# The low parts of eight heads' probabilities are transposed in two transfers of two blocks each instead of one of four

## The reference, cut to what matters

```python
q = split_heads(h @ Wq.T + bq)
k = split_heads(h @ Wk.T + bk)
v = split_heads(h @ Wv.T + bv)
scores = jnp.einsum('bhqd,bhkd->bhqk', q, k) * scale
scores = jnp.where(mask, -jnp.inf, scores)
attn = jax.nn.softmax(scores, axis=-1)
out = jnp.einsum('bhqk,bhkd->bhqd', attn, v)
out = out.transpose(0, 2, 1, 3).reshape(b, n, D_MODEL)
return out @ Wo.T + bo
```

## Time and profile before

| | us |
|---|---|
| median of 3 runs | 1293.63 |
| lowest, highest run | 1293.18, 1296.23 |
| the profiled execution | 1303.47 |
| its span in the trace | 1301.7 |

### The profile page before, as it was taken

The page is one execution under the profiler, slowest core; times in us unless marked ns, Lnnn a source line. Parts: engine busy times, 40 slices in busy tenths (PEclk is TensorE's granted clock), DMA queues, the critical chain, the costliest instruction groups (busy, mean ns, idle before and its releaser), DMA issues.

```text
span 1301.7 us, 39386 instructions
## 1 busy us (share of the span) xinstructions
PE 1163.3 (89%) x15385; PEld 966.6 (74%) x15385; DVE 1046.3 (80%) x2913; ACT 996.1 (77%) x2824; POOL 944.5 (73%) x1606
## 2 busy tenths in 40 slices
PE   3589999989999999999999999999999999999855
PEld 3367877777778777878777887778787788787743
DVE  3478888878888888888888888888888888888752
ACT  2367888788878878878887788778887888788652
POOL 1357777877877787778778777877787778777540
PEclk8689999999999999999999999999999999999996
DMA  5026656676766677766667666676566667665661
GB/s 179 9 50 107 118 114 119 138 123 120 128 131 131 119 135 131 127 120 137 130 110 131 134 129 131 122 132 130 120 134 131 131 120 134 131 130 111 119 115 48
DMA packets 508346, 156.52 MB, mean 120 GB/s; under 512 B 472064, under 2 KB 508160, under 8 KB 508160
## 3 DMA queue, kind: packets, MB, share of 16 engines
q1 hardware_dynamic: 508160, 154.00, 62.4%
HBM read 19.73 MB, written 16.78 MB: 28 GB/s over the span
## 4 chain that ended last, share of the span: by engine, by line
POOL 37%; DVE 24%; ACT 17%; PE 10%; DMA 8%; issue 4%; SPq 1%; POOLq 0%; DVEq 0%
DMA h_t<-h_rows 6%; ACT head_hi L1062 6%; POOL xn L1196 5%; POOL head_lo L1200 4%; POOL head_lo L1206 4%; POOL head_lo L1209 4%; POOL head_lo L1203 4%; DVE h_rows L889 3%; POOL rstd L1189 3%; ACT h_rows L1018 3%; DVE head_nmax L842 3%; DVE head_nmax L838 3%; DVE head_nmax L835 3%; POOL rstd L1220 3%; POOL xn L1193 3%
## 5 line engine op out<-in xcount | busy, mean ns | idle before, releaser
L385 PE MATMUL ps<-w_hi,h_t 128*128 128x256 f16 (+1 forms) x512 | 141.1, 276 | 7.8 <-DMA h_t<-h_rows 7.6
L386 PE MATMUL ps<-h_t,w_hi 128*128 128x256 f16 x512 | 140.9, 275 | 0.0
L387 PE MATMUL ps<-h_t,w_lo 128*128 128x256 f16 x512 | 140.8, 275 | 0.0
L385 PE MATMUL ps<-h_t,w_hi 128*128 128x256 f16 x512 | 140.8, 275 | 0.0
L386 PE MATMUL ps<-w_lo,h_t 128*128 128x256 f16 (+1 forms) x512 | 140.5, 274 | 0.0
L387 PE MATMUL ps<-w_hi,h_t 128*128 128x256 f16 (+1 forms) x512 | 140.2, 274 | 0.0
L385 PE MATMUL ps<-w_hi,agg_hi 128*128 128x256 f16 x512 | 140.1, 274 | 0.0
L386 PE MATMUL ps<-w_lo,agg_hi 128*128 128x256 f16 x512 | 139.7, 273 | 0.0
L387 PE MATMUL ps<-w_hi,agg_lo 128*128 128x256 f16 x512 | 139.4, 272 | 0.0
L1200 POOL TENSOR_TENSOR head_lo<-head_prob,head_hi 128x512 f16<-128x512 f32 x64 | 74.2, 1159 | 84.4 <-ACT head_hi L1062 84.4
L1062 ACT ACTIVATE head_hi<-head_prob 128x2048 f16<-128x2048 f32 x64 | 122.8, 1920 | 0.0
(11 more groups left out here) (192 smaller groups left out, 4956.2 us busy)
## 6 DMA issues: line engine op xcount, KB each, us to landing
x<-in_x SPq DMA_DIRECT2D x64, 256.0 KB, 3.1
out<-x SPq DMA_DIRECT2D x64, 256.0 KB, 2.7
h_t<-h_rows SPq DMA_TRANSPOSE x128, 3.1
head_t_hi<-head_hi SPq DMA_TRANSPOSE x64, 4.6
head_t_lo<-head_lo SPq DMA_TRANSPOSE x64, 4.3
mix_t<-mix_rows SPq DMA_TRANSPOSE x64, 3.0
w_f<-in_w SPq DMA_DIRECT2D x1, 256.0 KB, 2.8
w3t_f<-in_w_t SPq DMA_DIRECT2D x1, 256.0 KB, 3.1
```

Of the source, the lines that this page charges most:

```text
L385: pe.matmul(o, lh, rh, start=start, stop=False)
L386: pe.matmul(o, lh, rl, start=False, stop=False)
L387: return pe.matmul(o, ll, rh, start=False, stop=stop)
```

## The change

The one transfer of `head_lo` becomes two, each with a semaphore of its own. The first moves blocks 0 and 1 into the first eight tiles of `head_t_lo`, the second moves blocks 2 and 3 into the last eight. The first waits for `split_head_1_done`, as the one transfer did; the second has no wait and stands right behind it. PE's `head_sum_1` waits for three semaphores instead of two. POOL's list is the same, line by line.

```diff
-        move_heads_lo_done = [sem(f"move_heads_lo_done_{k}") for k in range(2)]
+        move_heads_lo_a_done = [sem(f"move_heads_lo_a_done_{k}") for k in range(2)]
+        move_heads_lo_b_done = [sem(f"move_heads_lo_b_done_{k}") for k in range(2)]
...
-            def move_heads_lo(g):
+            def move_heads_lo_a(g):
                 sp.wait_ge(split_head_1_done, g + 1)
-                sp.dma_start(head_t_lo[g % 2][:, :, :], head_lo[:, :, :].rearrange("p a n -> p (a n)"), transpose=True).then_inc(move_heads_lo_done[g % 2], 16)
+                sp.dma_start(head_t_lo[g % 2][:, 0:8, :], head_lo[:, 0:2, :].rearrange("p a n -> p (a n)"), transpose=True).then_inc(move_heads_lo_a_done[g % 2], 16)
+
+            def move_heads_lo_b(g):
+                sp.dma_start(head_t_lo[g % 2][:, 8:16, :], head_lo[:, 2:4, :].rearrange("p a n -> p (a n)"), transpose=True).then_inc(move_heads_lo_b_done[g % 2], 16)
...
                 at(4, move_heads_hi)
-                at(4, move_heads_lo)
+                at(4, move_heads_lo_a)
+                at(4, move_heads_lo_b)
...
                 pe.wait_ge(move_heads_hi_done[g % 2], 16 * (g // 2) + 16)
-                pe.wait_ge(move_heads_lo_done[g % 2], 16 * (g // 2) + 16)
+                pe.wait_ge(move_heads_lo_a_done[g % 2], 16 * (g // 2) + 16)
+                pe.wait_ge(move_heads_lo_b_done[g % 2], 16 * (g // 2) + 16)
```

## The result

| | us |
|---|---|
| before, median of 4 runs on the same chip | 1293.41 |
| after, median of 4 runs | 1314.15 (1313.36 to 1315.23) |
| ratio | 1.0156, 95% interval 1.0139 to 1.0174 |
| profiled execution of after, its span | 1315.23, 1313.4 |

The forecast was 1293.7 with a range up to 1299.0. The change costs 20.7 us, and it was put at 0.1. The two profiled executions are only 11.8 apart, since that of before was 9.8 above its median. So the traces are used for where the time goes, and the medians for how much.

A forecast was written before the change was run, and what follows sets the result against it. The prediction saw a ring of waits with POOL most often late. Cost 0 in 62 body groups, 2 x 0.05 = 0.1 in the last two, SP and PE 0, took 1293.63 to 1293.7, range 1290.5 to 1299.

The forecast's parts named there:

- What bounds the kernel: Whole kernel: a ring of waits, POOL most often late with 37% of the chain, all DMA landings 8%.
- The cover of 1.2 on PE: Head sums: low parts ready 1.2 to 1.4 before PE needs them; DVE adds 0.55 before POOL's wait is reached.
- No earlier start: First half's issue: still waits for POOL's fourth subtraction, so gain from overlap with the subtractions is 0.
- Issue on SP: SP's queue: two issues take 2.52, occupying SP 0.62 to 0.84 longer; move3's slack covers it, cost 0.
- The usual landing of the second half: Transfer of head_lo: second half lands 4.3 to 4.4 after the first half's issue, against 4.3 for the one transfer.
- Serial: Rival: second transpose moves nothing until the first lands, 6.1 after issue; +17, 1310.6 us; chance 0.05.
- +0.05: Second half's landing: the delay taken against the one transfer, with bounds from 0 or slightly less to +0.9.
- The third wait: PE's first head sum: a third semaphore wait costs 0, at most some hundredths of a us.
- 8 of the 62 landings come more than 0.6 late: Body groups in before: count used for the held-back rival, whose 0.9 delay passes 6.0 by about 0.1 each, 0.8 together.
- the permitted 6.0: Body groups: a landing costs time only when later than about 5.5 + 0.55, some 6.0, after the issue.
- a shift of the late landings: Rival: changed traffic moves coincidences of late move2 and move3 landings, 4 to 6 us either way, 1288 to 1299; chance 0.11.
- Held back like the high parts: Rival: second half lands at 5.2, +0.9, like the high parts behind other transfers; +2.6, 1296.2 us; chance 0.10.

The follow-up runs named there:

- the first experiment: The changed kernel with both halves counted on one semaphore, so PE has two waits before the head sums: 1312.33, ratio 1.0126 to before.
- whole with PE's packet outside: Kernel before plus 13 matmul pairs per slot and 64 at the start, holding PE's program packets away from the low parts' landing: 1284.08, ratio 0.9919.
- with whole: Kernel before plus 13 matmul pairs per slot and 26 at the start, holding PE's program packets inside the landing's stretch: 1283.11, ratio 0.9909.
- with split: Changed kernel plus 13 matmul pairs per slot and 26 at the start, holding PE's program packets inside the landing's stretch: 1334.66, ratio 1.0305.
- the extra half: Kernel before plus a 128x1024 transfer of constants behind the whole one, nobody waiting for it: 1313.93; with PE's packets held inside, 1327.40.

## Why the prediction was wrong

**What bounds the kernel.** Right. The cover of 1.2 on PE, that of 0.55 on DVE and POOL's wait behind them are the way that the late slots take.

**No earlier start.** Right: the first half is issued at 617.45, when the last subtraction ends.

**Issue on SP.** Right: 1.23 and 1.34 against 2 x 1.24. `move3` stands 4.17 behind the first issue and is not pushed.

**The usual landing of the second half.** Right in size: forecast 4.3 to 4.4 after the first half's issue, measured 4.4 to 4.5 where nothing disturbs. The "Serial" rival (6.1 in every group) is refuted by that: in 40 of 64 groups the two overlap. The Trainium skill's fixed cost per transfer (DMA: Bandwidth & Descriptors, section on the anatomy of one DMA), weighed in the prediction, is not paid twice in a row here: 4.5 for both against 2 x 3.1. One reading behind the +0.05 was loose. `move2` was said to land in 3.1 close behind `move_out`; that is the median of all slots, and in the slot of the earlier trace rows it took 3.5.

**The third wait.** Right, 0 (the first experiment).

**The late landings: the step that failed.** The forecast took "8 of the 62 landings come more than 0.6 late" from the trace of before (it is 7 of the 62, and the eighth is group 62) and carried it over, with at most 0.9 added to each. The sum then had a cost of 0 for 62 groups. In after, 24 of 64 second halves are 0.6 or more late, and they are at 5.8 to 6.7 instead of the permitted 6.0. In before, PE's packet starts in the same stretch in 25 groups, but a whole transfer lands 0.3 later for it, at 4.6, far inside its cover. So the count of late landings in before said nothing of how the new form would meet that packet. I had the late landings under my eyes, and didn't ask what they came from.

The trace shows something there that I overlooked. A second queue called "instruction", q14, has 65 packets of 8 KB in before and in after alike. In all eight late groups of before (4, 9, 17, 25, 38, 43, 56, 62) one of them starts 3.1 to 3.8 behind the last subtraction; in whole with PE's packet outside, all ten landings that are 0.6 or more late (none is over 5.3) have one at 3.7 to 3.9. Group 43 of before has no packet of q8 near; the landing, and window 892.1 to 898.6:

```profile
DMA to landing us min/median/max: 5.1/5.1/5.1
```
```profile
q14 instruction: 1, 0.01, 0.3%
```

In after, where such a packet comes without PE's (groups 4 and 43, at 2.8), the second half is in time, at 5.0 behind the last subtraction. So the eight landings that the forecast counted are marked by another packet than the 24 of after. That the packets of q14 are the cause is not shown: no run moves them, and in before three more groups (30, 35, 51) have one at 3.8 to 3.9 and land at 4.6 to 4.7. Shown is only that one is there at each late landing.

**The rival that came nearest** is "a shift of the late landings": right family, priced at 4 to 6 us from the spread of runs where 20.7 was true, and given 0.11. "Held back like the high parts" had the right sort of size for a delay (+0.9 where +1.2 to 2.1 was measured) but put it on the 8 groups only. The row for it was at hand: the high parts, which do follow close behind others, land as late as 6.3.

**A second term mis-sized.** Beyond 6.0 I counted only the excess, 0.1 per group. In after, the slot of a late group takes 19.21 by the median and that of a punctual one 18.47, so 0.7 is lost, and 1.3 at most. Of this, 0.44 is POOL's `norm2_1`, which goes from 1.06 to 1.50: in 21 of 23 late slots between groups 4 and 59, and in none of the 33 punctual ones. The same instruction has its median at 1.06 with whole and 1.50 with split, both with the packet inside; tile xn of each:

```profile
L1200 POOL TENSOR_SCALAR xn<-x,nmean,rstd x64: 554/1059/1499, 57.4 to 1219.4; 128x256 f32<-128x256 f32 x64
```
```profile
L1206 POOL TENSOR_SCALAR xn<-x,nmean,rstd x64: 554/1498/1506, 57.2 to 1273.0; 128x256 f32<-128x256 f32 x64
```

That the slot jumps by this is shown; why is open. The DVE instructions beside it are the same two in both slots above (lines 872 and 789 of after are lines 866 and 783 of before), only shifted against it, and in before it takes over 1.4 in 14 of 56 slots, without a late landing.

**What stays open.** Why seven groups of after have a packet in the stretch and land punctually. Why a packet of 0.95 us on one DMA engine costs a lone transfer 0.3 and one of a close pair 1.5 to 1.9. In the single groups read packet by packet, the last completion write of a whole transfer stood just ahead of the packet (3.94 and 3.95). In a late group of after the packet was at 4.2 and the last engine's completion write at 5.24, with the landing at 6.29, so there part of the loss is on the way to that write and part behind it. But in a late group with the extra half, the write was at 4.20, just ahead of the packet at 4.21, and the landing at 6.08. The Trainium skill (DMA: Bandwidth & Descriptors, section on queues, rings and completion order) says that the semaphore's write lands only after every earlier write of that engine, across its queues. This would let another queue's packet hold up a landing, but it explains neither sizes above the packet's own 0.95 nor why a lone transfer escapes; no run here tests it. Also open: single whole transfers that land at 6.0 and more (group 25 with the packets inside, and group 62 of before; both have a packet of q14 at 3.8 beside PE's, but so have groups 9, 17 and 56 of before, which land at 5.2), and why the profiled execution of before was 10 us above its median.

## What to carry to other kernels

Slack is not the deadline minus the median landing: count how many landings come late, ask what makes them late, and ask whether the new form of the transfer will meet the same thing worse. In these runs a transposing transfer with another one issued directly at it, waited for or not, was delayed much more by a packet of PE's program than one that stood alone (1.5 to 1.9 against 0.3). A split can win only where the first half can start earlier and somebody waits for the data; here neither was so. In a long unrolled loop like this one the fetch of PE's program is periodic DMA traffic that drifts against the loop: a change of some instructions can move it, so compare two variants at a held position (the loop's PE list padded to whole packets, 512 instructions here) before believing a difference of a per cent.

## What the runs showed of the hardware that I had not expected

- PE's program comes through the same DMA engines as the data, in packets of 16 KB, one per 253 to 254 PE instructions, each 0.93 to 0.96 us on one engine. They take 0.6% of the 16 engines' span, and where they fall decides between 1283.11 and 1295.54 for one and the same dataflow, and between 1286.91 and 1334.66 for the split one.
- With PE's packet inside, a transposing transfer for which nobody waits delays the one issued 1.95 us ahead of it: the landing goes from 4.6 to 6.1.
- Packets of 8 KB of a second instruction queue stand at every landing of before that is more than 0.6 late (eight of them, 4.9 to 6.1 after the issue instead of 4.3).
- 13 useless pairs per slot, 832 in all, cost nothing that can be seen and win 0.9% by their number alone; 6 per slot win nothing.
